# Moving two correlations and a transpose behind the convolutions on TensorE in a fused normalise, descriptor and convolution kernel

## The chip, the cores and the metric

One core of a Trainium2 chip runs the whole program as one launch. The metric is the device time of one execution in microseconds (us). The core's engines run their own instruction streams and wait for each other by semaphores: TensorE (PE in the rows, its weight loads PEld), VectorE (DVE), ScalarE (ACT), GpSimd (POOL) and SyncE (SP), which issues most of the transfers. In this measurement a difference below about 0.2% can't be told from no change.

## The reference, cut to what matters

```python
def _L0_conv_ref(x, W, bias):              # x is the group-normalised input, 16 x 512 x 64 x 64
    gs = spatial_descriptor(x, 5)          # 25 correlations of every pixel with its 5x5 neighbours
    norm = jnp.sqrt(jnp.sum(gs * gs, axis=1, keepdims=True) + EPS)
    gs = gs / norm
    feat = jnp.concatenate([x, gs], axis=1)
    out = jnp.einsum('bchw,oc->bohw', feat, W) + bias[None, :, None, None]
    return jax.nn.relu(out)
...
x = x + _L0_conv_ref(_gn(x), L0_conv_W, L0_conv_bias)
x = x + _L1_conv_ref(_gn(x), L1_conv_w1, L1_conv_b1, L1_conv_w2, L1_conv_b2)   # max pools mixed per plane
```

`_gn` subtracts the mean and divides by the spread of each of 32 groups of 16 channels. The change lies in the first of the two layers.

## The kernel before, in words

**Stages.** The first layer fills the first 60% of the time, the second (planes gathered by class, pooled on VectorE, mixed on TensorE) the rest. The change touches the first layer alone.

**Tiling.** An image (16 of them) is cut into `CH` = 8 chunks of 8 rows, 512 pixels. The 512 channels are `CT` = 4 tiles of 128, of the input and of the output. Each value is split into two halves, `gh` and `gl`, and a product takes three matmuls.

**TensorE per chunk c**, in the order in which `image` in the block of TensorE writes it:

- `picks` (L1245, 96 small matmuls): the 25 correlations of chunk c are picked from the masked blocks in `bq` into `BANK_A`. It waits for ScalarE's `after` of this chunk.
- `gram`, twice (L1198, 12 matmuls each here): correlations of pairs of rows for chunk c + 1. There are four of them to a chunk, in two PSUM banks in turn, so the third waits until VectorE's `mask` has read the first, the fourth until it has read the second (`s_masked`).
- `tail` (L1278): the descriptor's share of the convolution of chunk c - 1 is added into its four banks (one to an output tile).
- `norm` (L1268): the sum of squares for chunk c, into `BANK_N`.
- `gram`, twice more: the third and fourth.
- `conv` for output tile 0 (L1221 to L1223, 12 matmuls), `turn_blocks` (L1259, up to four transposes of blocks for the next chunk's picks, into `BANK_N`), then `conv` for tiles 1 to 3.

`conv(i, c, o)` writes the bank out of which ScalarE's `conv_out` must first have read output tile o of chunk c - 1, and waits for that by `s_relu`.

**ScalarE per chunk** (`image` in its block): two of four pieces of the chunk that lies three ahead are normalised (`normalise`, L580 and L582, freed by the last `conv` of the chunk before), then the square of the picks (L613), a third piece (L580, L582), the root of the norm (L617, behind `norm`), four `conv_out` of the chunk before (L594, behind `tail`), `after` (L601, reads the turned blocks), and the fourth piece. GpSimd makes the low half of each piece (`low_parts`, L438); the third piece waits until the low half of the first is made, since both use one buffer (`s_gl`). GpSimd also adds the residual (L447).

**VectorE per chunk**: statistics of the input two images on (`x_stats`, L741; twice in chunk 3, none in chunk 5), four masks (L791) with, between them, the descriptor (L833, L837) and statistics of the output (`y_stats`, L803), and then `wide_rows` (L812 to L827) of the chunk before. In chunk 4 (`STATS_AT`) the group statistics of the next image are worked out: `group_sums` (L751) behind the second mask, TensorE's `group_average` (L1286), `group_spreads` (L758 to L764), TensorE's `group_spread` (L1290), `group_values`.

All of this order is written out by hand; there is no planner.

Of the kernel before, what the change touches and what calls it, by code (L numbers as in the profile page):

```python
# [18 lines left out]
CT = C // P  # L19
ROWS = 8  # L20
CH = H // ROWS
CW = ROWS * W
NB = H // 2
PAIRS = ROWS // 2
# [62 lines left out]
def build(nc, x, wt, wturn, bias, w1t, b1, w2t, b2, consts, out):  # L87
# [21 lines left out]
    with ctx:  # L109
# [8 lines left out]
        o = 0  # L118
# [128 lines left out]
        s_vchain = sem("s_vchain")  # L247
# [7 lines left out]
        s_after = sem("s_after")  # L255
# [3 lines left out]
        s_root = sem("s_root")  # L259
# [51 lines left out]
        STATS_CHAIN = 7  # L311
        STATS_AT = 4
# [248 lines left out]
        def _(act):  # L561
# [5 lines left out]
            def normalise(i, c, cts=range(CT), first=False):  # L567

                n0 = (i * CH + c) * CT
                if 0 in cts:  # L570
                    act.wait_ge(s_newton, 3 * i + 3)
                    if not first:

                        act.wait_ge(s_chunk_used, i * CH + c - RING + 1)
                for ct in cts:
                    if not (isinstance(n0, int) and n0 + ct < 2):
                        act.wait_ge(s_gl, n0 + ct - 1)
                    act.sem_inc(s_carry_a, 1)
                    piece = xs(ct, c * CW, CW, i % 2)
                    act.activation(g32[:, ct % 2, :], piece, ACT.Identity, bias=gbias[:, ct:ct + 1],  # L580
                                   scale=grstd[:, ct:ct + 1])
                    act.activation(gh[:, ct, (c % RING) * CW:(c % RING + 1) * CW], piece, ACT.Identity,  # L582
                                   bias=gbias[:, ct:ct + 1], scale=grstd[:, ct:ct + 1]).then_inc(s_gh, 1)
# [19 lines left out]
            def image(i, last):  # L603
                for c in range(CH):
                    n = i * CH + c
                    first = isinstance(n, int) and n == 0

                    ahead = (i, c + 3) if c + 3 < CH else None if last else (i + 1, c + 3 - CH)
                    soon = ahead and c + 3 != CH
                    if soon:  # L610
                        normalise(*ahead, cts=(0, 1), first=first)
                    act.wait_ge(s_pick, n + 1)
                    act.activation(sq, psum[:, BANK_A, 0:QW], ACT.Square).then_inc(s_sq, 1)  # L613
                    if soon:
                        normalise(*ahead, cts=(2,))
                    act.wait_ge(s_norm, n + 1)
                    act.activation(sq, psum[:, BANK_N, 0:QW], ACT.Sqrt, bias=epsd[:, :]).then_inc(s_root, 1)  # L617
                    if not first:
                        for o in range(CT):
                            conv_out(n - 1, o)  # L620
                    if ahead and not soon:
                        normalise(*ahead, cts=(0, 1))
                    if c + 1 < CH:
                        after(i, c + 1)
                    elif not last:
                        after(i + 1, 0)
                    if ahead:
                        normalise(*ahead, cts=(3,) if soon else (2, 3))
                    if c == STATS_AT and not last:
                        group_root(i + 1)  # L630

# [87 lines left out]
        def _(dve):  # L719
# [34 lines left out]
            def group_spreads(i):  # L754
                b = i * STATS_CHAIN
                dve.wait_ge(s_xagg, 2 * i + 1)
                dve.wait_ge(s_gavg, 2 * i + 1)
                dve.tensor_copy(gm[:, :], psum[:, BANK_N, 0:CT]).then_inc(s_vchain, 1)  # L758
                dve.wait_ge(s_vchain, b + 2)
                dve.tensor_tensor(gd[:, :], aggx[:, :, 0], gm[:, :], ALU.subtract).then_inc(s_vchain, 1)  # L760
                dve.wait_ge(s_vchain, b + 3)
                dve.tensor_tensor(gd[:, :], gd[:, :], gd[:, :], ALU.mult).then_inc(s_vchain, 1)
                dve.wait_ge(s_vchain, b + 4)
                dve.tensor_tensor(gd[:, :], gd[:, :], aggx[:, :, 1], ALU.add).then_inc(s_xagg, 1)  # L764
# [65 lines left out]
            def descriptor(i, c):  # L830
                n = i * CH + c
                dve.wait_ge(s_root, n + 1)
                dve.reciprocal(sq, sq).then_inc(s_rinv, 1)  # L833
                dve.wait_ge(s_rinv, n + 1)
                if not (isinstance(n, int) and n == 0):
                    dve.wait_ge(s_t, n)
                dve.tensor_tensor(fn, psum[:, BANK_A, 0:QW], sq, ALU.mult).then_inc(s_fn, 1)  # L837
# [9 lines left out]
            def image(i, first=False, left=2):  # L847

                last = left == 0
                for c in range(CH):  # L850
                    if c > 0:
                        res = [lambda o=o: y_stats(i, c - 1, o) for o in range(CT)]
                    elif first:
                        res = []
                    else:
                        res = [lambda o=o: y_stats(i - 1, CH - 1, o) for o in range(CT)]
                    sums = [lambda: group_sums(i + 1)] if c == STATS_AT and not last else []
                    between = [[], sums + [lambda: descriptor(i, c)], res[0:1], res[1:4]]
                    if c == 0 and first:
                        x_stats(1, 0)  # L860
                        x_stats(1, 1)
                    if c < 5 and left >= 1:
                        x_stats(i + 1, c + 2 if c < 4 else CH - 1)
                    elif c > 5 and left >= 2:
                        x_stats(i + 2, c - 6)
                    if c + 1 < CH:
                        masks_of(i, c + 1, between)
                    elif not last:
                        masks_of(i + 1, 0, between)
                    else:  # L870
                        for fs_ in between:
                            for f in fs_:
                                f()
                    if c == 0 and not first:
                        keep_stats(i - 1)
                    if c == 3 and left >= 1:
                        x_stats(i + 1, CH - 2)
                    if c > 0:
                        wide_rows(i, c - 1)
                    elif not first:  # L880
                        wide_rows(i - 1, CH - 1)
                    if c == STATS_AT and not last:
                        group_spreads(i + 1)
                        group_values(i + 1)

            def keep_stats(i):
# [309 lines left out]
        def _(pe):  # L1196
# [85 lines left out]
            def group_average(i):  # L1282
                pe.wait_ge(s_xagg, 2 * i + 1)
                if not (isinstance(i, int) and i == 0):
                    pe.wait_ge(s_after, (i - 1) * CH + STATS_AT + 2)
                pe.matmul(psum[:, BANK_N, 0:CT], gavg, aggx[:, :, 0], start=True, stop=True).then_inc(s_gavg, 1)  # L1286

            def group_spread(i):
                pe.wait_ge(s_xagg, 2 * i + 2)
                pe.matmul(psum[:, BANK_N, CT:2 * CT], gavg, gd[:, :], start=True, stop=True).then_inc(s_gavg, 1)  # L1290

            def image(i, last):
                for c in range(CH):

                    nxt = (i, c + 1) if c + 1 < CH else None if last else (i + 1, 0)
                    convs = list(range(CT))
                    picks(i, c)
                    if nxt:

                        pe.wait_ge(s_gl, (i * CH + min(c + 3, CH)) * CT if c + 1 < CH else ((i + 1) * CH + 2) * CT)  # L1300
                        gram(nxt[0], PAIRS * nxt[1])
                        gram(nxt[0], PAIRS * nxt[1] + 1)
                    if c:
                        tail(i, c - 1)
                    elif not (isinstance(i, int) and i == 0):
                        tail(i - 1, CH - 1)
                    norm(i, c, last)
                    if nxt:
                        gram(nxt[0], PAIRS * nxt[1] + 2)
                        gram(nxt[0], PAIRS * nxt[1] + 3)  # L1310
                        conv(i, c, convs.pop(0))
                        turn_blocks(*nxt)
                    for n, o in enumerate(convs):
                        conv(i, c, o)
                        if c == STATS_AT and not last and n == 0:
                            group_average(i + 1)
                    if c == STATS_AT and not last:
                        group_spread(i + 1)

# [115 lines left out]
```

## Time and profile before

| what | us |
|---|---|
| runs shown, median (lowest to highest of 3) | 4111.97 (4111.73 to 4114.0) |
| profiled execution, its own time | 4115.68 |
| its span in the trace | 4113.9 |
| TensorE busy | 3403.6 (83%) |
| VectorE busy | 3392.5 (82%) |
| GpSimd busy | 2080.1 (51%) |
| ScalarE busy | 1971.2 (48%) |

The profiled execution is 1.8 us longer than its span, and 3.7 us longer than the median of the runs. Shares over the whole span mix two layers with different limits, so they are read for each stage.

### The profile page before, as it was taken

How to read it: one execution, taken by the hardware profiler on the slowest of the kernel's cores; microseconds unless marked ns; L12 is line 12 of the kernel's file. 1: busy time of each engine (PE TensorE's matmuls, PEld its weight loads, DVE VectorE, ACT ScalarE, POOL GpSimd, SP SyncE). 2: the span in 40 equal slices, each digit the busy share in tenths (PEclk: the TensorE clock that was granted, in tenths of full speed). 3: DMA queues.
4: the chain of work that ended last, by engine and by line, in shares of the span. 5: the costliest groups of instructions: out<-in, count | busy, mean ns of one | idle time of the engine just before them, and what ended most of it. 6: DMA issues, size and time to landing. Idle time of an engine off the chain costs nothing. (4 is left out here: it accounts for less than half of the span.)

```text
span 4113.9 us, 83924 instructions
## 1 busy us (share of the span) xinstructions
PE 3403.6 (83%) x28232; PEld 1926.1 (47%) x28233; DVE 3392.5 (82%) x3619; ACT 1971.2 (48%) x3219; POOL 2080.1 (51%) x1564
## 2 busy tenths in 40 slices
PE   5999999999999999999999996465666666877665
PEld 3665665565655655665655664122222222333222
DVE  6877777777777777777777766899999999999997
ACT  4544545545545545445545540334444445554566
POOL 4555555555546546556555551345455544454443
PEclk9999999999999999999999996677888888998888
DMA  5454444454445445454454334464565666864466
GB/s 194 162 187 162 167 173 171 169 176 165 160 168 183 160 172 179 161 175 175 167 175 169 129 121 85 172 235 182 226 246 229 265 257 236 338 271 169 182 250 242
DMA packets 251672, 782.36 MB, mean 190 GB/s; under 512 B 97433, under 2 KB 97433, under 8 KB 229273
## 3 DMA queue, kind: packets, MB, share of 16 engines
q1 hardware_dynamic: 219600, 417.47, 29.2%
q0 software_dynamic: 31568, 358.89, 22.2%
q8 instruction: 228, 3.74, 0.4%
q14 instruction: 276, 2.26, 0.2%
HBM read 421.55 MB, written 409.08 MB: 202 GB/s over the span
## 5 line engine op out<-in xcount | busy, mean ns | idle before, releaser
L1041 DVE TENSOR_TENSOR arena<-arena 128x2048 f32<-128x2048 f32 (+8 forms) x635 | 1454.8, 2319 | 57.2 <-DMA arena<-wide_planes,arena 13.8
L438 POOL TENSOR_TENSOR arena<-arena 128x512 f16<-128x512 f32 x512 | 652.4, 1279 | 883.8 <-ACT arena L582 883.5
L1395 PE MATMUL psum<-arena 128*128 128x512 f32 x896 | 532.8, 680 | 465.2 <-issue 313.7
L1198 PE MATMUL psum<-arena 128*128 128x256 f16 (+1 forms) x6344 | 731.1, 274 | 81.5 <-DVE arena L791 61.0
L1221 PE MATMUL psum<-arena 128*128 128x512 f16 x2048 | 777.3, 380 | 1.0 <-ACT arena L594 1.0
L1222 PE MATMUL psum<-arena 128*128 128x512 f16 x2048 | 777.0, 379 | 0.0
L1223 PE MATMUL psum<-arena 128*128 128x512 f16 x2048 | 776.9, 379 | 0.0
L447 POOL TENSOR_TENSOR arena<-arena 128x512 f32 (+1 forms) x512 | 639.6, 1270 | 226.6 <-ACT arena L594 221.7
L580 ACT ACTIVATE arena<-arena,gbias,grstd 128x512 f32 (+1 forms) x512 | 413.7, 808 | 637.3 <-PE psum L1223 527.6
L1198 PEld LDWEIGHTS psum<-arena 128*128 128x128 f16 x6344 | 597.4, 100 | 175.2 <-DVE arena L791 68.5
L1397 PE MATMUL psum<-arena 128*128 128x512 f32 x1072 | 601.6, 659 | 57.0 <-ACT psum L667 47.9
L681 ACT ACTIVATE arena<-psum 128x512 f32<-128x512 f32 x536 | 314.2, 599 | 689.6 <-PE psum L1397 680.4
L803 DVE BATCH_NORM_STATS2 bny<-arena 128x6 f32 (+1 forms) x512 | 351.4, 690 | 266.6 <-POOL arena L447 262.1
L530 POOL DMA_INDIRECT out<-arena x67 | 183.9, 2745 | 747.3 <-issue 747.3
L1395 PEld LDWEIGHTS psum<-arena 128*128 128x128 f32 x896 | 188.4, 217 | 725.2 <-issue 546.3
L594 ACT ACTIVATE arena<-psum,bias_sb 128x512 f32<-128x512 f32 x512 | 337.2, 684 | 219.7 <-POOL arena L447 207.4
L582 ACT ACTIVATE arena<-arena,gbias,grstd 128x512 f16 (+1 forms) x512 | 409.4, 800 | 0.0
L667 ACT ACTIVATE psum<-arena 128x512 f32<-128x512 f32 x536 | 383.1, 766 | 48.6 <-ACT arena L681 47.5
L1397 PEld LDWEIGHTS psum<-arena 128*128 128x128 f32 x1072 | 230.2, 216 | 371.3 <-issue 307.8
L791 DVE TENSOR_TENSOR arena<-psum,cst 128x256 f32<-128x256 f32 x496 | 280.6, 589 | 108.4 <-PE psum L1198 108.3
L741 DVE BATCH_NORM_STATS2 bnx<-arena 128x6 f32 (+1 forms) x512 | 315.1, 680 | 29.5 <-issue 20.7
L1223 PEld LDWEIGHTS psum<-arena 128*128 128x128 f16 x2048 | 200.3, 98 | 241.9 <-issue 0.3
(151 smaller groups left out, 3085.8 us busy)
## 6 DMA issues: line engine op xcount, KB each, us to landing
arena<-in_x SPq DMA_DIRECT2D x64, 2048.0 KB, 13.2
wide_planes<-arena SPq DMA_DIRECT2D x128, 1024.0 KB, 9.3
y_planes<-arena SPq DMA_DIRECT2D x64, 2048.0 KB, 7.8
arena<-arena SPq DMA_DIRECT2D x1536, 8.0 KB, 1.8
arena<-wide_planes,arena POOLq DMA_INDIRECT x69, 11.6
arena<-plane_records,arena POOLq DMA_INDIRECT x67, 7.7
arena<-y_planes,arena POOLq DMA_INDIRECT x67, 9.8
out<-arena POOLq DMA_INDIRECT x67, 9.2
```

The lines of the kernel that those rows point to most:

```text
L438: pool.tensor_tensor(gl[:, ct, slot], g32[:, ct % 2, :], gh[:, ct, slot], ALU.subtract).then_inc(s_gl, 1)
L447: pool.tensor_tensor(y, y, relu[:, o % 2, :], ALU.add).then_inc(s_added, 1)
L580: act.activation(g32[:, ct % 2, :], piece, ACT.Identity, bias=gbias[:, ct:ct + 1], scale=grstd[:, ct:ct + 1])
L582: act.activation(gh[:, ct, (c % RING) * CW:(c % RING + 1) * CW], piece, ACT.Identity, bias=gbias[:, ct:ct + 1], scale=grstd[:, ct:ct + 1]) ...
L667: act.activation(psum[:, b, :], bufs[:, u, b * CW:(b + 1) * CW], ACT.Identity, bias=recs_in[:, u, 3:4], scale=recs_in[:, u, 0:1]).then_inc ...
L1041: ins = dve.tensor_tensor(dst, a, b, ALU.max)
L1198: return pe.matmul(dst, w, m, start=(k == 0), stop=(k == nk - 1))
L1221: pe.matmul(dst, h, gh[:, ct, slot], start=(ct == 0), stop=False)
L1222: pe.matmul(dst, h, gl[:, ct, slot], start=False, stop=False)
L1223: last = pe.matmul(dst, l, gh[:, ct, slot], start=False, stop=(ct == CT - 1))
L1395: pe.matmul(dst, diag[:, s, 0, :], small[:, s, b * ROWS:(b + 1) * ROWS, 1:W + 1], start=False, stop=False, skip_group_check=True)
L1397: pe.matmul(dst, diag[:, s, 1, :], big[:, s, b * CW:(b + 1) * CW], start=False, stop=True, skip_group_check=True).then_inc(s_mix, 1)
```

## The change

On TensorE the third `gram` of the next chunk goes behind `conv` of output tile 0, the fourth behind `conv` of tile 1, and `turn_blocks` behind `conv` of tile 2. `conv` of tile 0 so stands directly behind `norm`. In chunk 4 `group_average` stands behind `conv` of tile 0 (it was behind tile 1), and `group_spreads` on VectorE goes from behind `wide_rows` to behind the third mask. On ScalarE the fourth piece is normalised ahead of `after`. Two waits are set to match: `group_average` waits for the root, `group_spread` for `after`, and `turn_blocks` in chunk 4 for the copy of the group's mean.

```diff
@@ ScalarE, image
                         normalise(*ahead, cts=(0, 1))
+                    if ahead:
+                        normalise(*ahead, cts=(3,) if soon else (2, 3))
                     if c + 1 < CH:
                         after(i, c + 1)
                     elif not last:
                         after(i + 1, 0)
-                    if ahead:
-                        normalise(*ahead, cts=(3,) if soon else (2, 3))
@@ VectorE, image
-                    between = [[], sums + [lambda: descriptor(i, c)], res[0:1], res[1:4]]
+                    spreads = [lambda: group_spreads(i + 1)] if c == STATS_AT and not last else []
+                    between = [[], sums + [lambda: descriptor(i, c)], spreads + res[0:1], res[1:4]]
...
                     if c == STATS_AT and not last:
-                        group_spreads(i + 1)
                         group_values(i + 1)
@@ TensorE, group_average and group_spread
-                    pe.wait_ge(s_after, (i - 1) * CH + STATS_AT + 2)
+                    pe.wait_ge(s_root, (i - 1) * CH + STATS_AT + 1)
...
+                if not (isinstance(i, int) and i == 0):
+                    pe.wait_ge(s_after, (i - 1) * CH + STATS_AT + 2)
@@ TensorE, image
                     norm(i, c, last)
-                    if nxt:
-                        gram(nxt[0], PAIRS * nxt[1] + 2)
-                        gram(nxt[0], PAIRS * nxt[1] + 3)
-                        conv(i, c, convs.pop(0))
-                        turn_blocks(*nxt)
-                    for n, o in enumerate(convs):
+                    for o in range(CT):
                         conv(i, c, o)
-                        if c == STATS_AT and not last and n == 0:
+                        if c == STATS_AT and not last and o == 0:
                             group_average(i + 1)
+                        if nxt and o < 2:
+                            gram(nxt[0], PAIRS * nxt[1] + 2 + o)
+                        if nxt and o == 2:
+                            if c == STATS_AT and not last:
+                                pe.wait_ge(s_vchain, (i + 1) * STATS_CHAIN + 2)
+                            turn_blocks(*nxt)
```

On TensorE, from the tail of chunk 4 on, the rows of before are these (L1198 are the third and fourth correlation, L1221 is the first matmul of the convolution of tile 0; the words in brackets name the semaphores that a row waits for):

```order
L1278 MATMUL psum<-arena 128x4x64x2 [waits grouped1]
L1278 MATMUL psum<-arena 128x4x64x2 x3
L1268 MATMUL psum<-arena,cst 128x128 [waits s_sq]
L1198 MATMUL psum<-arena 128x256 [waits s_masked]
L1198 MATMUL psum<-arena 128x256 x11
L1198 MATMUL psum<-arena 128x256 [waits s_masked]
L1198 MATMUL psum<-arena 128x256 x11
L1221 MATMUL psum<-arena 128x512 [waits s_relu]
```

At the same place of the changed kernel, TensorE has this:

```order
L1278 MATMUL psum<-arena 128x4x64x2 [waits grouped1]
L1278 MATMUL psum<-arena 128x4x64x2 x3
L1268 MATMUL psum<-arena,cst 128x128 [waits s_sq]
L1221 MATMUL psum<-arena 128x512 [waits s_relu]
L1222 MATMUL psum<-arena 128x512
L1223 MATMUL psum<-arena 128x512
```

The row that waits for `s_relu` stood behind 24 matmuls of the correlations and now stands directly behind the norm. Further on in the same chunk, at the end of the convolution of tile 0, TensorE of the changed kernel has this (L1286 is `group_average`, which stands there in chunk 4 alone; the last row is the first of the convolution of tile 1):

```order
L1222 MATMUL psum<-arena 128x512
L1223 MATMUL psum<-arena 128x512
L1286 MATMUL psum<-aggx,cst 128x4 [waits s_root,s_xagg]
L1198 MATMUL psum<-arena 128x256 [waits s_masked]
L1198 MATMUL psum<-arena 128x256 x11
L1221 MATMUL psum<-arena 128x512 [waits s_relu]
```

The third correlation has come behind tile 0, and in chunk 4 the wait for VectorE's sums (`s_xagg`) has come ahead of it. On VectorE, in chunk 4, the difference is this piece (L791 is a mask, L803 `y_stats`, L824 and L827 end `wide_rows`):

```order
 L837 TENSOR_TENSOR arena<-psum,arena 128x128
 L791 TENSOR_TENSOR arena<-psum,cst 128x2x16x8
+L758 COPY gm<-psum 128x4
+L760 TENSOR_TENSOR gd<-aggx,gm 128x4
+L762 TENSOR_TENSOR gd<-gd 128x4
+L764 TENSOR_TENSOR gd<-gd,aggx 128x4
 L803 BN_STATS bny<-arena 128x6
 L791 TENSOR_TENSOR arena<-psum,cst 128x2x16x8
```

The four small operations of `group_spreads` have come ahead of the fourth mask; they stood behind L827.

## Rows read from the trace of the kernel before

**Rows 1.** The page: busy time, share of the span and instructions by engine.
```profile
PE 3403.6 (83%) x28232; PEld 1926.1 (47%) x28233; DVE 3392.5 (82%) x3619; ACT 1971.2 (48%) x3219; POOL 2080.1 (51%) x1564
```

**Rows 2.** One line's instructions, the picks: duration ns min/median/max, first and last start us.
```profile
L1245 PE MATMUL psum<-arena,cst x12288: 182/196/219, 54.8 to 2486.5; 128*32 128x32 f32 x181, 128*32 128x24 f32 x18
```

**Rows 3.** Waits of PE up to 2560 us: us in total, times, longest us.
```profile
PE psum L1198 <- DVE arena L791: 61.0, 39, 5.3
...
PE psum L1290 <- DVE gd L764: 18.1, 16, 1.2
```

**Rows 4.** Timeline of PE, chunk 7 and the start of chunk 0 behind it.
```profile
1417.23 1.03 PE L1245 MATMUL psum<-arena,cst 128*32 128x32 f32 x96
...
1421.74 0.39 PE L1268 MATMUL psum<-arena,cst 128*128 128x128 f32 x2
1421.96 2.78 PE L1198 MATMUL psum<-arena 128*128 128x256 f16 x24
1424.59 0.38 PE L1221 MATMUL psum<-arena 128*128 128x512 f16 x1
...
1427.17 0.60 PE L1259 MATMUL psum<-cst,arena 128*128 128x128 f32 x4
...
1435.47 1.02 PE L1245 MATMUL psum<-arena,cst 128*32 128x24 f32 x96
...
1445.29 4.22 PE L1198 MATMUL psum<-arena 128*128 128x256 f16 x24 [4.93 <-DVE arena L791]
```

**Rows 5.** Timeline of all engines, the last chunk of the last image.
```profile
2487.54 0.39 PE L1268 MATMUL psum<-arena,cst 128*128 128x128 f32 x2
...
2488.23 1.26 ACT L594 ACTIVATE arena<-psum,bias_sb 128x512 f32<-128x512 f32 x2
...
2488.97 0.39 PE L1221 MATMUL psum<-arena 128*128 128x512 f16 x1 [1.04 <-ACT arena L594]
```

**Rows 6.** Timeline of ACT in the chunk of rows 4.
```profile
1422.75 1.26 ACT L594 ACTIVATE arena<-psum,bias_sb 128x512 f32<-128x512 f32 x2 [0.22 <-issue]
```

**Rows 7.** Timeline of DVE in the chunk of rows 4 and behind it.
```profile
1425.91 0.58 DVE L791 TENSOR_TENSOR arena<-psum,cst 128x256 f32<-128x256 f32 x1
...
1435.15 1.23 DVE L819 TENSOR_TENSOR arena<-arena 128x1024 f32<-128x1024 f32 x1 [2.86 <-DMA wide_planes<-arena]
...
1442.28 2.47 DVE L741 BATCH_NORM_STATS2 bnx<-arena 128x6 f32 x4 [1.15 <-issue]
```

**Rows 8.** Timeline of all engines in a chunk 6.
```profile
1555.70 1.20 DVE L827 TENSOR_TENSOR arena<-arena 128x992 f32<-128x992 f32 x1 [0.22 <-DVE arena L824]
...
1556.16 2.87 POOL L438 TENSOR_TENSOR arena<-arena 128x512 f16<-128x512 f32 x2 [1.88 <-ACT arena L582]
...
1558.16 0.81 ACT L580 ACTIVATE arena<-arena,gbias,grstd 128x512 f32 x1 [0.51 <-POOL arena L438]
1558.62 0.39 PE L1268 MATMUL psum<-arena,cst 128*128 128x128 f32 x2
...
1559.76 1.16 POOL L438 TENSOR_TENSOR arena<-arena 128x512 f16<-128x512 f32 x1 [0.74 <-ACT arena L582]
...
1559.84 0.67 ACT L594 ACTIVATE arena<-psum,bias_sb 128x512 f32<-128x512 f32 x1
```

**Rows 9.** Timeline of DVE, end of a chunk 3 and start of chunk 4.
```profile
1356.60 1.17 DVE L812 TENSOR_TENSOR arena<-arena 128x992 f32 x1
...
1362.24 2.47 DVE L741 BATCH_NORM_STATS2 bnx<-arena 128x6 f32 x4
1364.62 1.02 DVE L791 TENSOR_TENSOR arena<-psum,cst 128x256 f32<-128x256 f32 x2
1365.48 1.04 DVE L751 BATCH_NORM_AGGREGATE aggx<-bnx 128x2 f32<-128x48 f32 x4
```

**Rows 10.** Windows: busy us (x instructions) of PE, PEld, DVE, ACT, POOL, then PEclk, DMA share, GB/s.
```profile
1283.50:1287.00 3.50, 1.44 (x56) 1.17 (x45) 3.25 (x3) 3.33 (x6) 1.99 (x2) 1.00 0.01 3
1444.80:1448.20 3.40, 2.91 (x14) 2.11 (x15) 2.06 (x5) 0.51 (x1) 0.98 (x3) 0.51 0.10 36
```

More of the change, by code:

```diff
@@ L1295, in image @@
                     nxt = (i, c + 1) if c + 1 < CH else None if last else (i + 1, 0)
-                    convs = list(range(CT))
                     picks(i, c)
```

## The prediction

> **What bounds the kernel now.** The shares of busy time come first: TensorE at 83% and VectorE at 82% leave open which of them leads [rows 1], so the first layer, where the change lies, is read by itself. There the picks mark the chunks: 12288 matmuls are 128 chunks of 96, the first starts at 54.8 us, the last at 2486.5 us and, being the end of its group, about 0.8 us behind the group's start. So 127 chunks take 2431 us, 19.14 us each [rows 2]. The timeline of TensorE then shows a chunk in which nothing is waited for: from the picks at 1417.23 to those at 1435.47 is 18.24 us, all of it filled [rows 4]. TensorE is the bound, and what a chunk takes above 18.24 us is all that an order of its work can win: 0.90 us in the mean, 115 us in all.
>
> The waits of TensorE say where that is: 61.0 us in 39 waits of a correlation for VectorE's mask, and 18.1 us of the spread's matmul for VectorE (once an image) [rows 3]. The longest kind is the third correlation at 1445.29, after 4.93 us of idling; behind it 24 matmuls take 4.22 us instead of 2.78 [rows 4], at a granted clock of 0.51 [rows 10]: 1.4 us more, on top of the wait. That is the 1.2 GHz level, after an idle engine. 115 - 61 - 18 leaves some 35 us, mostly such stretches at the low clock. The reader is to see one more thing in rows 4: of its own next work TensorE never waits in this chunk, since the 24 matmuls of the third and fourth correlation (2.63 us from 1421.96 to 1424.59) lie between the norm and the first convolution.
>
> **The change part by part.** No instruction is added but waits; all costs and gains are of order.
>
> *Removed, up to 114 us.* The third correlation comes 2.58 us later in TensorE's stream (tile 0's convolution, 1424.59 to 1427.17 [rows 4]) and the spread's matmul finds its input made before `wide_rows`. The gain's bounds are all three sums, 114 us, and 75 us if the long wait of chunk 0 (4.93 us) and the low clock behind it only halve: some 2.5 us of 15 images. Why I take the whole: VectorE's fourth mask now follows the fourth correlation, and all of `wide_rows` moves with it. Counted from a chunk's picks: norm at 4.51, convolution of tile 0 at 4.73 plus the new wait (1.5, below), then 2.58 + 1.31 + 2.58 + 1.31 and 0.16 for the modelled end: the fourth mask starts at 14.2 us (before: 1425.91 - 1417.23 = 8.7 [rows 7]). A mask (0.6), three statistics (1.85, from four in 2.47) and the 5.64 us from L812 to the next L741 (1356.60 to 1362.24 [rows 9]) end `wide_rows` at 22.3 to 22.4, with a chunk of 19.74 us: 2.7 us into the next. That is later than before, but the 2.86 us that L819 waited for a store, until 1435.15 = 17.9 us into chunk 7 [rows 7], go: L819 is wanted at 18.2 now (14.2 + 0.6 + 1.85 and about 1.5 for what stands between, L812's 1.17 [rows 9] among it). In chunk 0, with the 1.15 us at VectorE's loop and 2.47 us of input statistics [rows 7], the first mask ends at 2.7 + 1.15 + 2.47 + 0.6 = 6.9 us; the third correlation wants it at 4.73 + 1.5 + 2.58 = 8.8. Cover of 1.9 us; what is late next if it is gone is this correlation again.
>
> *Added: tile 0's convolution waits for ScalarE, in 126 chunks.* Its bank is free when `conv_out` of tile 0 of the chunk before has read it. ScalarE does that behind the root, which needs the norm, and the tail that writes this bank stands just ahead of the norm too. In the order before, the two correlations hid this. One chunk shows it bare: the last of all, where no correlations follow. The norm starts at 2487.54, the convolution at 2488.97, 1.43 us later, and the row names ScalarE's L594 as what it waited for [rows 5]. Where work follows at once, the next matmul starts 0.22 us behind the norm's start (1421.74 to 1421.96 [rows 4]). The new wait is 1.43 - 0.22 = 1.21 us at least, since ScalarE was idle there. In the chunk of rows 4 the first L594 starts at 1422.75 [rows 6]; one alone takes 0.67 [rows 8], and the convolution followed its end by 0.07 [rows 5]: 1423.49, against the slot at 1421.96: 1.53 us. In a chunk 6 it is 1559.84 + 0.67 + 0.07 against 1558.84: 1.74 us, as ScalarE's third piece waited 0.51 us for GpSimd, whose two low halves took 2.87 us there and not twice the 1.16 of the next, beside VectorE's L827, which ended at 1556.90 [rows 8]. That is 2.8 us behind this chunk's picks (4.51 ahead of the norm: 1554.11), and by the count above L827 now ends 2.7 us behind them in most chunks. So six chunks of eight should be near 1.6 us, chunk 5 (no piece ahead of the norm) near 1.25, chunk 4 (`wide_rows` so late that the first low half goes before its last steps) near 1.25: a mean of 1.5 us. 126 x 1.5 = 189 us; bounds 126 x 1.21 = 152 and 126 x 1.74 = 219. (The first chunk has no such wait, the last has it already.)
>
> The Trainium skill, SBUF — State Buffer, section "SBUF: two separate sides", has the shared port of VectorE and GpSimd as an exclusive lock: with two inputs in SBUF on VectorE, the later of the two is blocked until the other ends. The 2.87 us agree. By the page's rule in its full length, a low half that comes just after L827's start would be held 1.2 us, and the sum would be 126 x 0.5 us, some 60 us, higher.
>
> *Added: chunk 4 waits for the group sums.* `group_average` now stands ahead of the third correlation and needs L751, which needs VectorE to be through. Chunk 3 has input statistics twice, so there `wide_rows` ends at 2.7 + 2.4 = 5.1 us into chunk 4, up to 1.8 us later where it shares time with GpSimd's low halves. Then 2.4 us of L741, 1.0 of two masks and 1.04 of L751 [rows 9]: 9.5 to 11.3 us. TensorE is there at 4.73 + 1.25 + 2.58 = 8.6. I take 2 us: 15 x 2 = 30 us; bounds 0 and 45.
>
> *At nothing.* `turn_blocks` later: it ends at about 17 us of 19.7, `after` (one read of a bank, like a `conv_out`'s 0.67 [rows 8]; ScalarE has its fourth piece done by then) lies under tile 3's convolution of 2.58 us. Were that cover gone, the picks would wait for it in full. The transfers that regroup the descriptor for the next tail hang on L837, which comes up to 3 us later behind the masks; their use is a chunk away, so I cost them at nothing and keep them as a thing that could go wrong. The second layer is not touched.
>
> **Sum**, on the profiled execution's 4115.7 us: -114 + 189 + 30 = +105, 4220.7 us. The median of the runs is 3.7 us below that execution: 4217 us.
>
> **The rivals.**
>
> *Faster: the wait is hidden after all.* It would need ScalarE to have read tile 0's bank when the norm is issued. With no wait the sum is -114 + 30 = -84: 4028 us. It decides at 84 / 126 = 0.67 us a chunk; below that the change wins. For it: ScalarE is busy for 48% [rows 1]. Against: with ScalarE idle the bare wait was 1.21 us [rows 5], and its order of root and `conv_out` stays. 0.05.
>
> *No change that can be measured* (0.2% is 8 us): gain and wait cancel at 0.6 to 0.7 us a chunk, 4112 us. Against it the same row. 0.03.
>
> *Much slower: the pauses bring the clock down.* If each chunk's pause were followed by a stretch at the low level that costs 1.4 us, as in rows 10, 126 x 1.4 = 176 us come on top: 4393 us. Against it: TensorE was busy for 1.44 of 3.50 us at 1283.50, after which the clock still read 1.00 [rows 10]; the low clock stands behind a pause of 4.93 us. 0.04. The Trainium skill, TensorE: Matmul & The Clock Gate, section "A second HAM failure mode: psum-queue depth-cycling", speaks for it: short pauses between groups of matmuls made the clock swing between its levels. No run here shows that for pauses below 2 us.
>
> *Slower by more, through VectorE and GpSimd holding each other up:* each low half held in full, the wait near 2 us in six chunks of eight, about 126 x 0.4 = 50 us on top, with the long wait of chunk 0 half kept (39): near 4305 us. For it: rows 8, and that `wide_rows` now ends beside the low halves in nearly every chunk. Against: L827 (1.20 us) has run for 0.46 us when the first low half starts [rows 8], so at most the rest of it is lost. 0.08.
>
> **How the numbers follow.** My forecast, slower by 40 to 165 us, has 0.80; the rivals 0.05, 0.03, 0.04 and 0.08. The bounds give 152 - 114 + 0 = +38 and 219 - 75 + 45 = +189, that is 4150 and 4301. I cut the upper one, where all ends meet, to 4275, and leave out the clock's rival and the faster side: 4150 to 4275. Faster 0.05, same 0.03, slower 0.92.
>
> **What would show it.** In the changed profile: waits of L1221 for ScalarE's L594, some 126 of 1.2 to 1.75 us; no long waits of L1198 for L791; a chunk near 19.7 us; L1286 waiting for L751 about 2 us in 15 images; the spread's matmul not waiting; fewer stretches at the low clock; the third piece (L580) waiting for L438 in most chunks. Wrong would be: no waits on L594 (then the bank was free), a clock that falls in each chunk, or a TensorE that waits for the tail's transfers.

## The result: slower by 3.2%, and the profile after

The changed kernel takes 4243.6 us in the median of 4 runs (4242.5 to 4253.6), the kernel before 4113.0 us (4111.7 to 4118.2): a ratio of 1.0321, 95% interval 1.0303 to 1.0339. The forecast was 4217 us, within 4150 to 4275.

The profiled execution of the changed kernel took 4242.53 us. Beside [rows 1], TensorE's busy time on the page has grown by 20 us and VectorE's has fallen, so no engine has more to do; the time is idle time:

```profile
PE 3423.7 (81%) x28232; PEld 1925.9 (45%) x28233; DVE 3335.4 (79%) x3619; ACT 1969.4 (46%) x3219; POOL 2082.1 (49%) x1564
```

The picks again mark the chunks. As in [rows 2], the line's instructions of the changed kernel, first and last start at the end of the numbers:

```profile
L1245 PE MATMUL psum<-arena,cst x12288: 183/196/218, 55.0 to 2610.0; 128*32 128x32 f32 x181, 128*32 128x24 f32 x18
```

From the first pick to the last are 2555.0 us, against 2431.7 before: 123.3 of the 126.9 us between the two profiled executions (4242.53 - 4115.68) are lost in the first layer. The waits of TensorE in it, beside [rows 3] (us in total, times, longest, up to 2700 us):

```profile
PE psum L1221 <- ACT arena L594: 154.1, 127, 1.7
PE psum L1286 <- DVE aggx L751: 71.6, 16, 30.7
...
PE psum L1292 <- DVE gd L764: 0.9, 1, 0.9
```

No row of L1198 waiting for L791 is left of the 61.0 us in 39 waits, and the spread's matmul (now L1292) has 0.9 of 18.1 us. In their place stand 127 waits of a convolution for ScalarE, and L1286 waiting for L751: one of 30.7 us at the start, which the kernel before has too, and 15 of 40.9 us together. A plain chunk of the changed kernel on TensorE's timeline:

```profile
1383.27 1.03 PE L1245 MATMUL psum<-arena,cst 128*32 128x32 f32 x96
...
1387.77 0.39 PE L1268 MATMUL psum<-arena,cst 128*128 128x128 f32 x2
1389.33 0.39 PE L1221 MATMUL psum<-arena 128*128 128x512 f16 x1 [1.17 <-ACT arena L594]
...
1391.93 1.47 PE L1198 MATMUL psum<-arena 128*128 128x256 f16 x12
```

The convolution starts 1.56 us behind the norm's start; work that needs no wait started 0.22 behind it [rows 4]. So the wait costs 1.34 us, of which 1.17 show as idling: the other 0.17 is the next matmul's lead over the norm's end. The last of the 127 waits (1.0 us) was there before; what idling shows as 153 us in the 126 new ones costs about 153 + 126 x 0.17, some 174 us. Chunk 4, on the same timeline:

```profile
1428.50 0.39 PE L1221 MATMUL psum<-arena 128*128 128x512 f16 x1 [1.08 <-ACT arena L594]
...
1434.24 0.38 PE L1286 MATMUL psum<-aggx,cst 128*128 128x4 f32 x2 [2.98 <-DVE aggx L751]
...
1436.16 0.63 PE L1221 MATMUL psum<-arena 128*128 128x512 f16 x1
```

and the window that follows (columns as in [rows 10], the seventh number PEclk):

```profile
1436.00:1440.00 4.00, 4.00 (x14) 1.65 (x13) 3.47 (x6) 0.00 (x0) 3.96 (x4) 0.65 0.05 10
```

A convolution's matmul takes 0.63 us there and not 0.38: the granted clock went down towards the 1.2 GHz level behind the pause of 2.98 us, where before it came in chunk 0 [rows 4, 10]. By the clock records of the two traces the first layer has 58 us at that level in the kernel before (13 stretches) and 44 us in the changed kernel (10, nine of them behind this wait of chunk 4).

VectorE's timeline, in the chunk before that plain chunk (chunk 1) and into the plain one (chunk 2), answers to [rows 7]:

```profile
1366.00 1.17 DVE L824 TENSOR_TENSOR arena<-arena 128x32 f32<-128x32 f32 x1
1367.39 1.87 DVE L827 TENSOR_TENSOR arena<-arena 128x992 f32<-128x992 f32 x1 [0.21 <-DVE arena L824]
...
1377.76 0.60 DVE L791 TENSOR_TENSOR arena<-psum,cst 128x256 f32<-128x256 f32 x1 [2.79 <-PE psum L1198]
1378.20 1.85 DVE L803 BATCH_NORM_STATS2 bny<-arena 128x6 f32 x3
...
1384.05 0.23 DVE L824 TENSOR_TENSOR arena<-arena 128x32 f32<-128x32 f32 x1
1384.47 1.20 DVE L827 TENSOR_TENSOR arena<-arena 128x992 f32<-128x992 f32 x1 [0.20 <-DVE arena L824]
```

VectorE stands idle for 2.79 us in front of the fourth mask, with three output statistics queued behind it, and `wide_rows` ends at 1385.67, 2.4 us into the next chunk. In the chunk before that it ended only at 1369.26, 6.0 us in (the picks of that chunk start at 1363.23), and GpSimd and ScalarE show it:

```profile
1365.26 2.95 POOL L438 TENSOR_TENSOR arena<-arena 128x512 f16<-128x512 f32 x2 [8.37 <-ACT arena L582]
...
1385.30 2.57 POOL L438 TENSOR_TENSOR arena<-arena 128x512 f16<-128x512 f32 x2 [6.89 <-ACT arena L582]
```

```profile
1367.35 0.81 ACT L580 ACTIVATE arena<-arena,gbias,grstd 128x512 f32 x1 [0.59 <-POOL arena L438]
```

Two low halves took 2.95 us beside L824 and L827, against 2.57 in the plain chunk, and the third piece waited 0.59 us for the first of them. That is chunk 1 of each image; it carries the longest wait for ScalarE, near 1.6 us.

### The profile page after: what moved, and what is told of

Its sections match the earlier page's. It is cut to its first block and busy times, and to the rows that moved or that the text cites. A ratio compares the mean times of both kernels' runs of the same rounds, so it can differ in the third digit from the quotient of the medians.

```text
span 4240.7 us, 83953 instructions
## 1 busy us (share of the span) xinstructions
PE 3423.7 (81%) x28232; PEld 1925.9 (45%) x28233; DVE 3335.4 (79%) x3619; ACT 1969.4 (46%) x3219; POOL 2082.1 (49%) x1564
## 5 line engine op out<-in xcount | busy, mean ns | idle before, releaser
L438 POOL TENSOR_TENSOR arena<-arena 128x512 f16<-128x512 f32 x512 | 649.0, 1272 | 926.0 <-ACT arena L582 925.2
L1221 PE MATMUL psum<-arena 128*128 128x512 f16 x2048 | 782.0, 382 | 154.1 <-ACT arena L594 154.1
L1223 PE MATMUL psum<-arena 128*128 128x512 f16 x2048 | 778.9, 380 | 0.0
L447 POOL TENSOR_TENSOR arena<-arena 128x512 f32 (+1 forms) x512 | 650.8, 1292 | 246.4 <-ACT arena L594 243.9
L1198 PE MATMUL psum<-arena 128*128 128x256 f16 (+1 forms) x6344 | 738.4, 271 | 16.2 <-POOL arena L438 11.4
L791 DVE TENSOR_TENSOR arena<-psum,cst 128x256 f32<-128x256 f32 x496 | 275.4, 591 | 604.2 <-PE psum L1198 602.2
L1198 PEld LDWEIGHTS psum<-arena 128*128 128x128 f16 x6344 | 595.2, 99 | 147.7 <-POOL arena L438 11.5
L580 ACT ACTIVATE arena<-arena,gbias,grstd 128x512 f32 (+1 forms) x512 | 413.4, 807 | 292.6 <-PE psum L1223 256.8
L601 ACT ACTIVATE arena<-psum 128x512 f32<-128x512 f32 (+1 forms) x128 | 74.7, 584 | 740.8 <-PE psum L1259 740.8
L1221 PEld LDWEIGHTS psum<-arena 128*128 128x128 f16 x2048 | 201.2, 98 | 364.5 <-ACT arena L594 178.0
```

Of the source, the lines that this page charges most:

```text
L438: pool.tensor_tensor(gl[:, ct, slot], g32[:, ct % 2, :], gh[:, ct, slot], ALU.subtract).then_inc(s_gl, 1)
L447: pool.tensor_tensor(y, y, relu[:, o % 2, :], ALU.add).then_inc(s_added, 1)
L1198: return pe.matmul(dst, w, m, start=(k == 0), stop=(k == nk - 1))
L1221: pe.matmul(dst, h, gh[:, ct, slot], start=(ct == 0), stop=False)
L1223: last = pe.matmul(dst, l, gh[:, ct, slot], start=False, stop=(ct == CT - 1))
```

## The experiments

Ten kernels ran, three rounds each, each against the kernel before on the same chip. Theory A is that of the forecast: the loss is the late release of tile 0's bank, and beside it the group's chain in chunk 4. Theory B makes VectorE's later work the cause and the waits only its show. Theory C, formed on the way, is the queue behind the fourth mask. All diffs are against the changed kernel, but where said.

### e1: the group's average behind tile 1 again

```diff
-                        if c == STATS_AT and not last and o == 0:
+                        if c == STATS_AT and not last and o == 1:
                             group_average(i + 1)
```

> The changed kernel, but group_average in chunk 4 goes back behind the convolution of tile 1. Theory A (most of the loss is the wait of tile 0's convolution for ScalarE's read of its bank, 127 waits; the wait for the group sums in chunk 4 and the low clock behind it are a second, separate loss): the 41 us of waits for L751 and some 15 us of low clock behind them go, 4175 to 4200 us against 4243. Theory B (VectorE's later work is the cause, and the waits only show it): the lateness comes out at another row, 4230 to 4250 us.

Measured: 4210.0 us, ratio 1.0224 (1.0207 to 1.0241), so 34 us of the 131 came back, outside both ranges: A had 43 to 68 us, B 14 at most. The waits say why:

```profile
PE psum L1221 <- ACT arena L594: 153.5, 127, 1.6
...
PE psum L1198 <- DVE arena L791: 20.4, 13, 1.6
...
PE psum L1259 <- DVE arena L791: 4.4, 15, 0.7
```

The 40.9 us for L751 went, and 25 us of waits for masks came at the third correlation and the transposes: in chunk 4 VectorE is late for whatever asks first. The low clock behind the wait went too: by the clock records 7 us of it are left of 44, which at half speed is worth some 19 us. 41 - 25 + 19 is 35, against the 34 us. The 127 waits for ScalarE did not move.

### e2: the third correlation directly behind the norm

```diff
                     norm(i, c, last)
+                    if nxt:
+                        gram(nxt[0], PAIRS * nxt[1] + 2)
                     for o in range(CT):
                         conv(i, c, o)
...
-                        if nxt and o < 2:
-                            gram(nxt[0], PAIRS * nxt[1] + 2 + o)
+                        if nxt and o == 0:
+                            gram(nxt[0], PAIRS * nxt[1] + 3)
```

> The changed kernel, but the third correlation goes back directly behind the norm (fourth behind tile 0, transposes behind tile 2 as in the change). Theory A: its 1.31 us cover nearly all of the 1.37 us a chunk, so some 150 us come back, while the third correlation's wait for the mask in chunk 0 returns in part (3 us and the low clock behind it, 15 times): 4100 to 4160 us. Theory B (VectorE's later work is the cause): the waits move from L594 to the masks, 4210 us or more.

Measured: 4081.4 us, ratio 0.9913 (0.9897 to 0.993): better than A foresaw, and faster than the kernel before. Its waits:

```profile
PE psum L1198 <- DVE arena L791: 53.4, 40, 3.9
...
PE psum L1221 <- ACT arena L594: 1.0, 1, 1.0
```

One correlation of 1.31 us is cover enough: of the 127 waits for ScalarE the one of the last chunk is left, as in the kernel before. The waits for masks are back, 53.4 us, less than the 61.0 before.

### e6: the change without its move of the correlations

```diff
                     norm(i, c, last)
+                    if nxt:
+                        gram(nxt[0], PAIRS * nxt[1] + 2)
+                        gram(nxt[0], PAIRS * nxt[1] + 3)
                     for o in range(CT):
                         conv(i, c, o)
...
-                        if nxt and o < 2:
-                            gram(nxt[0], PAIRS * nxt[1] + 2 + o)
```

> The change without its move of the correlations: both stand directly behind the norm again, while the transposes stay behind tile 2, the group's average behind tile 0, its spreads ahead of the fourth mask, and ScalarE's fourth piece ahead of its copy. Theory A: the 17 us of the spread's wait go and nothing is lost, 4085 to 4105 us, so the whole loss of the change belongs to the place of the correlations. Rival (the transposes' place or the group's chain costs): 4125 us or more.

Measured: 4085.0 us, ratio 0.9936 (0.9914 to 0.9958), on the lower edge of what A foresaw. All else in the change (transposes, average, spreads, ScalarE's fourth piece) is worth about 28 us of gain; the place of the correlations alone costs 4243.6 - 4085.0 = 159 us. That is a net sum: with the correlations back, `group_average` comes later and does not wait either, and 54.3 us of waits for masks are back, so 174 + 41 - 54 = 161 us stand against the 159.

### e3: ScalarE reads tile 0's bank ahead of the root

```diff
                     act.activation(sq, psum[:, BANK_A, 0:QW], ACT.Square).then_inc(s_sq, 1)
+                    if not first:
+                        conv_out(n - 1, 0)
...
-                        for o in range(CT):
+                        for o in range(1, CT):
                             conv_out(n - 1, o)
```

> The changed kernel, but ScalarE reads tile 0's bank (conv_out of tile 0) directly behind the square, ahead of the third piece and the root. Theory A: the wait of tile 0's convolution falls from 1.37 to 0.1 or 0.2 us a chunk, 150 us come back, VectorE's reserve shrinks and costs 0 to 20 us in chunks 0 and 4: 4085 to 4115 us. Theory B: VectorE loses the 1.3 us a chunk that the waits gave it, and waits for its masks take their place: above 4190 us.

Measured: 4164.1 us, ratio 1.0115 (1.0098 to 1.0133): 79 us back, half of what A foresaw and more than B allowed. TensorE's timeline (the line numbers are two higher here: L1270 is the norm, L1223 the convolution):

```profile
1210.51 0.39 PE L1270 MATMUL psum<-arena,cst 128*128 128x128 f32 x2
1210.99 0.39 PE L1223 MATMUL psum<-arena 128*128 128x512 f16 x1
```

The convolution starts 0.48 us behind the norm and not 1.56, so the wait that is left costs 0.26 us a chunk, 33 us in all, and some 140 of the 174 us are gone. They are not all won, as the waits for VectorE (L1288 is `group_average`, L1200 a correlation; from 60 us on) show:

```profile
PE psum L1288 <- DVE aggx L753: 47.7, 15, 3.3
...
PE psum L1200 <- DVE arena L793: 33.7, 25, 3.0
```

81 us against 41 in the changed kernel; the low clock covers 54 us against 44, and the rest of the 61 us that were not won is not accounted for. Both theories missed. Two causes of the new waits stand open. One is B's: the pauses had also given VectorE 1.3 us a chunk. The other lies in the edit: ScalarE's root now stands behind the read and the third piece. In the chunk shown here it starts 1.73 us behind the norm's start, in the plain chunk of the changed kernel 0.59 us (1388.36 against 1387.77). ScalarE's two rows, this kernel's first:

```profile
1212.24 0.35 ACT L619 ACTIVATE arena<-psum,epsd 128x128 f32<-128x128 f32 x1
```

```profile
1388.36 0.35 ACT L617 ACTIVATE arena<-psum,epsd 128x128 f32<-128x128 f32 x1
```

VectorE's descriptor waits for this root. e3 does not part the two causes; e5 and e10 bear on it.

### e5: the same move of ScalarE's in the kernel before

The diff is that of e3, made in the kernel before and with nothing else.

> The kernel before, with ScalarE's read of tile 0's bank moved ahead of the root and nothing else. Theory A (the bank's late release costs only where a convolution stands right behind the norm): nothing waits for it here, so no change, 4105 to 4125 us. If ScalarE's order by itself were worth time (the descriptor later by 0.6 us, or pieces later): more than 10 us off.

Measured: 4180.5 us, ratio 1.0157 (1.013 to 1.0183): 67 us slower where A expected nothing. VectorE's waits for ScalarE's root, of the kernel before and of this one, over the first layer:

```profile
DVE arena L833 <- ACT arena L617: 74.0, 84, 1.2
```

```profile
DVE arena L835 <- ACT arena L619: 175.5, 100, 3.7
```

The root comes later behind `conv_out`, the descriptor waits for it, and in the old order the third and fourth masks stand ready behind the descriptor. TensorE waits 80.2 us for masks at the correlations against 61.0, and 21 us at the transposes against 0.7; the low clock covers 109 us against 58, worth some 25 us. Together that is 65 of the 67 us. ScalarE's order is no free variable, and e3, e4, e7, e9 and e10 all carry this edit. In e3 it should cost less, since there VectorE's masks wait 429 us for their correlations anyway (101 in the kernel before); how much it costs there was not tried.

### e4: e1 and e3 together

Both diffs above, on the changed kernel.

> Both edits on the changed kernel: tile 0's bank read ahead of the root, and group_average behind tile 1. Theory A: 150 and 55 us come back, 4020 to 4060 us, so below the kernel before (4113), as the waits for masks that the change takes away stay away. Theory B: 4110 us or more.

Measured: 4116.4 us, ratio 0.9998 (0.9985 to 1.0011). Missed by 56 us at least: 60.3 us of waits for masks in 40 waits are back, as many as in the kernel before. VectorE is late again; whether for want of the pauses (B) or through the later root, this run does not say.

### e8: three output statistics ahead of the fourth mask

```diff
-                    between = [[], sums + [lambda: descriptor(i, c)], spreads + res[0:1], res[1:4]]
+                    between = [[], sums + [lambda: descriptor(i, c)], spreads + res[0:4], []]
```

> The changed kernel with the same three statistics ahead of the fourth mask. Theory C: the wait for the group sums in chunk 4 falls from 2.7 to about 0.8 us and the low clock behind it goes; in chunks 1 and 7 the wait for ScalarE falls from 1.6 and 1.4 to 1.1 us, as wide_rows no longer meets GpSimd's first low half: 4175 to 4205 us. The waits for ScalarE stay (127, near 1.1 us each). Rival (VectorE's lateness comes from elsewhere): 4230 us or more.

Measured: 4192.4 us, ratio 1.0188 (1.0166 to 1.0209), as C foresaw. The waits:

```profile
PE psum L1221 <- ACT arena L594: 152.6, 127, 1.8
```

L1286 waits no longer but at the start. So the wait for the group sums came from the queue that the change put behind the fourth mask. The rows of `wide_rows` at the start of chunk 4 show how, the changed kernel's first (picks at 1422.49), then e8's (picks at 1396.96):

```profile
1424.56 2.17 DVE L822 TENSOR_TENSOR arena<-arena 128x992 f32<-128x992 f32 x1 [0.22 <-DVE arena L819]
1426.65 1.17 DVE L824 TENSOR_TENSOR arena<-arena 128x32 f32<-128x32 f32 x1
1428.04 1.87 DVE L827 TENSOR_TENSOR arena<-arena 128x992 f32<-128x992 f32 x1 [0.22 <-DVE arena L824]
```

```profile
1397.23 1.22 DVE L822 TENSOR_TENSOR arena<-arena 128x992 f32<-128x992 f32 x1 [0.22 <-DVE arena L819]
1398.35 0.23 DVE L824 TENSOR_TENSOR arena<-arena 128x32 f32<-128x32 f32 x1
1398.80 1.19 DVE L827 TENSOR_TENSOR arena<-arena 128x992 f32<-128x992 f32 x1 [0.22 <-DVE arena L824]
```

With 1.85 us of statistics moved ahead, L822 and L824 end and L827 begins before GpSimd starts its first low half there (1399.00), so the three operations are 2.6 us shorter as well. The part on chunks 1 and 7 did not hold: the waits for ScalarE stay at 152.6 us in all.

### e7 and e9: the statistics early, with ScalarE's read early

e7 is e4 with the edit of e8, e9 is e3 with it.

> Tile 0's bank read early and the average late (as e4), and VectorE takes the last three output statistics ahead of the fourth mask, where it stands idle for 2.8 us, not behind it. Theory C (what came back in e4 is VectorE's work queued behind the fourth mask, which the change moved 5.5 us back): wide_rows ends 1.9 us earlier, of the 60 us of waits for masks some 40 go: 4055 to 4090 us. Rival (the store of wide planes and the loop hold VectorE in chunk 0, not its queue): 4100 us or more.

> The changed kernel with tile 0's bank read ahead of the root (as e3) and the three statistics ahead of the fourth mask (as e8); the group's average stays behind tile 0. Theory C: the two losses are the late bank and VectorE's queue behind the fourth mask, and with both taken away a chunk is 18.5 us, chunk 4 near 20 and chunk 0 near 20.6: 4075 to 4100 us, below the kernel before by some 0.7%. Rival (with the wait for ScalarE gone VectorE is late whatever its order): 4110 us or more.

Measured: e7 4118.8 us, ratio 1.0009 (0.9999 to 1.0018); e9 4115.7 us, ratio 1.001 (0.9999 to 1.0022). Both missed. e7's rows first, then e9's (from 60 us on; L1261 are the transposes):

```profile
PE psum L1200 <- DVE arena L793: 28.8, 26, 2.8
PE psum L1261 <- DVE arena L793: 28.5, 14, 2.1
```

```profile
PE psum L1288 <- DVE aggx L753: 30.6, 15, 2.3
...
PE psum L1200 <- DVE arena L793: 17.1, 12, 2.4
```

In e7 the waits of the correlations did halve, but in chunk 4 the spreads wait for the late average and hold the fourth mask, and the transposes wait 2 us for it: my own edit made that wait. In e9 chunk 4 still waits 2 us for the sums: in this order VectorE's reserve there is too small. Theory C, as far as it said that the bank and the queue are all that is lost, does not hold.

### e10: e9 with the tail ahead of the first two correlations

```diff
                     picks(i, c)
+                    if c:
+                        tail(i, c - 1)
+                    elif not (isinstance(i, int) and i == 0):
+                        tail(i - 1, CH - 1)
                     if nxt:
...
-                    if c:
-                        tail(i, c - 1)
-                    elif not (isinstance(i, int) and i == 0):
-                        tail(i - 1, CH - 1)
                     norm(i, c, last)
```

> As e9, with the tail ahead of the first two correlations, so that tile 0's bank is written 2.6 us earlier and ScalarE, which reads it behind the square, no longer holds the convolution by 0.1 us of idling and 0.16 of filling a chunk. Theory A: that 0.26 us times 126 go in part, as VectorE loses them too: 4050 to 4085 us. Rival (the tail now waits for the regrouping transfers, or ScalarE's third piece is delayed): e9's time or up to 40 us above it.

Measured: 4053.9 us, ratio 0.9857 (0.9836 to 0.9879), the fastest of all. TensorE's timeline around the norm:

```profile
1007.87 1.04 PE L1280 MATMUL psum<-arena 96*128 96x512 f16 x4
1008.74 2.79 PE L1200 MATMUL psum<-arena 128*128 128x256 f16 x24
1011.36 0.39 PE L1270 MATMUL psum<-arena,cst 128*128 128x128 f32 x2
1011.59 0.38 PE L1223 MATMUL psum<-arena 128*128 128x512 f16 x1
```

The convolution follows the norm by 0.23 us: no wait, with the correlations where the change puts them. The waits that are left in the first layer:

```profile
PE psum L1280 <- DMA arena<-arena: 25.9, 36, 1.7
...
PE psum L1288 <- DVE aggx L753: 11.9, 11, 1.2
```

The tail now waits for the regrouping transfers in part of the chunks, as the rival said, but for 25.9 us. 62 us between e9 and e10 are more than the 33 us of the 0.26 us a chunk; chunk 4's wait fell by 19 us as well, and the low clock from 44 to 7 us. ScalarE has its root earlier (0.95 us behind the norm's start in this chunk, 1012.31 against 1011.36), and VectorE's waits for it fell, e9's row first, then e10's:

```profile
DVE arena L835 <- ACT arena L619: 116.5, 96, 2.6
```

```profile
DVE arena L835 <- ACT arena L619: 19.2, 37, 2.6
```

So TensorE, which in this kernel has no wait for ScalarE's reads of the banks, waits for VectorE less than in the changed kernel: 21 us for the sums and the masks together (at the transposes too), against 41 there, 81 in e3, 64 in e4 and 51 in e9. The want of the pauses alone does not make VectorE late. The later root of those kernels is the likelier cause, but it was not tried by itself.

## Why the prediction was right

*The added wait* was there, in its place and with the releaser named: 127 waits, 126 of them new, about 174 us in all against 189 forecast (152 to 219). The mean was 1.4 us and not 1.5. The step that set six chunks of eight near 1.6 us was too high: `wide_rows` ended 2.4 us into a chunk (forecast 2.7), and the low halves were held for 0.25 us there. The sign that the third piece would wait for L438 in most chunks did not come: L580 waits for it 33 times in the 127 chunks, where the kernel before has 69 waits. Chunk 1 was not seen apart: chunk 0 has two operations more on VectorE (`keep_stats`, 1.9 us), and `wide_rows` then meets the low halves (1.6 us more in L824 and L827), so it ends 6.0 us into chunk 1, and there the third piece did wait. e2 and e6 show that this wait is the loss: a correlation between norm and convolution, and it is gone.

*The group sums* cost 40.9 us of waits against 30 forecast (0 to 45), 2.7 us an image for 2. The sums were ready 11.6 us into chunk 4, the forecast had 9.5 to 11.3: it allowed 1.8 us for meeting the low halves, and the rows under e8 show 2.6. e8 also shows what made VectorE late.

*The removed waits* were forecast at -114 us: 61 and 18 came (61.0 and 17.2), most of the 35 us of the low clock did not. 123.3 is 174 + 41 - 61 - 17 less some 13 us, so by this reckoning about 13 of the 35 were won; the clock records (58 us at half speed before, 44 after) give 7 of them, and the other 6 are not accounted for. That is the step that was off: I let the low clock go with chunk 0's wait and did not put a price on the one that the wait in chunk 4 would bring, though the row of such a pause stood before me [rows 10]. e1 takes the wait in chunk 4 away, and with it all but 7 us of the low clock go. These terms, +22 for the clock, +11 for the sums and -15 for the bank, with 3.6 us outside the first layer, are the 22 us between the forecast and the measured difference. That the total came so near is in part luck, since two terms were too kind and one too harsh.

*The rivals.* The faster one fell: the bank was never free at the norm. The one with the clock brought down by each pause fell too: in e1, with 127 pauses of 1.04 to 1.65 us and few longer ones, the window from 60 to 2400 us reads a granted clock of 1.00, where the kernel before has 0.99:

```profile
60.00:2400.00 2340.00, 2167.94 (x23930) 1339.32 (x23928) 1674.19 (x2620) 1108.59 (x1773) 1258.73 (x1174) 1.00 0.46 161
```

What the Trainium skill, TensorE: Matmul & The Clock Gate, "A second HAM failure mode: psum-queue depth-cycling", says of short pauses between groups is not borne out here for pauses of this length. The lock of the shared port (the Trainium skill, SBUF — State Buffer, "SBUF: two separate sides") agrees with chunk 1: L824 takes 1.17 us beside a low half, where it takes 0.23 us in the plain chunk, at 1384.05. That each low half would be held in full did not come.

*At nothing* was right for the transposes and `after`: picks wait for neither. That the change leaves VectorE reserve came true. The forecast counted this reserve with the pause in it and did not say so. Whether it needs the pause is open: e3, e4 and e9 take the pauses away and the masks are late again, but they also make the root later; e10 has neither pauses nor late masks.

## What to carry to other kernels

Before filler work is moved away from the place between two dependent steps, look up what the next instruction waits for and when that comes: here 1.31 us of correlation hid the read of a bank, and with that one correlation back in its place 162 us came back (e2). The gain of a wait that is taken out is the difference to the next limit, and an edit that takes it out can bring that limit nearer: e3 took away some 140 us and kept 79, and it made the root later on the way. A queue of ready work behind an instruction that waits (the statistics behind the fourth mask) is worth looking for on each engine: it cost 51 us here (e8). Reordered together with the bank's early release and the tail, the moved correlations gave 4053.9 us, 1.4% below the kernel before.

## What the runs showed that I had not expected

The move of one 0.67 us read on ScalarE, which nothing on TensorE waits for in the kernel before, made it 67 us slower (e5); by the waits in its trace this went through a root that came later and a descriptor that VectorE had in its queue ahead of two masks. And the granted clock read 1.00 with 127 pauses of 1.04 to 1.65 us in e1, but fell to 0.65 behind one of 2.98 us in the changed kernel. Even that pause did not do it each time: of the 13 images whose wait in chunk 4 is 2.92 to 3.02 us, nine show slow convolution matmuls behind it, and the two with the longest, 3.02 us, do not.
